# Attention: each row's maximum brought into its row of q by DMA through DRAM in place of transposes and copies, scores 18 pairs of units ahead of the keys in place of 13

## What is computed

```
q, k, v = ...                                   # (4, 12, 513, 16), from a projection of the tokens
a = jax.nn.softmax(jnp.einsum('bhnd,bhmd->bhnm', q, k) * scale, axis=-1)
o = jnp.einsum('bhnm,bhmd->bhnd', a, v)
```

## Time and profile before

| | |
|---|---|
| median of 3 runs | 1972.85 us (1969.68 to 1983.47) |
| the profiled execution | 1996.65 us, span 1994.9 us |
| busy in the span | PE 1500.4, DVE 1375.3, ACT 1074.7, POOL 315.6 us |
| attention in the second layer | about 890.7 to 1077.3 us of the span |
| attention in the last layer | about 1631 to 1817.6 us of the span |
| granted TensorE clock, mean of the span | 0.82 |

### The profile page before, as it was taken

The page is one execution under the profiler, slowest core; times in us unless marked ns, Lnnn a source line. Parts: engine busy times, 40 slices in busy tenths (PEclk is TensorE's granted clock), DMA queues, the critical chain, the costliest instruction groups (busy, mean ns, idle before and its releaser), DMA issues. The chain is left out here.

```text
span 1994.9 us, 35648 instructions
## 1 busy us (share of the span) xinstructions
PE 1500.4 (75%) x13740; PEld 1117.2 (56%) x13740; DVE 1375.3 (69%) x2930; ACT 1074.7 (54%) x1862; POOL 315.6 (16%) x396
## 2 busy tenths in 40 slices
PE   5899993954499849599998504888059599998596
PEld 5888992954366627464445503877047454445274
DVE  6988984798457545649994676776465559993466
ACT  7988992322545326347985425555000438894365
POOL 0000000002567210120000102776000220000100
PEclk9999995876558759698997656999578789997598
DMA  4111001000000010000000333111100000000100
GB/s 128 37 49 33 2 1 44 1 4 1 1 1 1 7 30 1 9 1 1 2 2 5 104 96 110 55 57 52 65 13 0 10 1 2 2 2 4 30 1 32
DMA packets 44499, 49.78 MB, mean 25 GB/s; under 512 B 11000, under 2 KB 37334, under 8 KB 44332
## 3 DMA queue, kind: packets, MB, share of 16 engines
q1 hardware_dynamic: 38354, 32.61, 5.8%
q0 software_dynamic: 3840, 9.18, 1.5%
q10 hardware_dynamic: 2138, 5.72, 1.2%
HBM read 38.32 MB, written 9.19 MB: 24 GB/s over the span
## 5 line engine op out<-in xcount | busy, mean ns | idle before, releaser
L1879 DVE TENSOR_REDUCE att_max<-banks 104x1 f32<-104x512 f32 (+1 forms) x480 | 296.0, 682 | 15.4 <-PE banks L1794 11.3
L1914 ACT ACTIVATE att_p<-banks 104x514 f32<-104x514 f32 (+1 forms) x480 | 261.8, 599 | 35.6 <-PE banks L1837 25.5
L332 PE MATMUL banks<-tok_wT,feature_halves 128*128 128x192 f16 x2592 | 228.0, 248 | 23.4 <-DVE feature_halves L358 12.3
L332 PEld LDWEIGHTS banks<-tok_wT,feature_halves 128*128 128x128 f16 x2592 | 216.0, 99 | 32.4 <-DVE feature_halves L358 18.1
L1853 PE MATMUL banks<-att_p,att_v 104*32 104x257 f32 (+1 forms) x1920 | 163.1, 413 | 0.6
L1837 PE MATMUL banks<-att_q,att_kT 64*104 64x257 f16 (+1 forms) x960 | 156.2, 307 | 2.6 <-ACT att_p L1914 2.5
L1794 PE MATMUL banks<-att_kT,att_q 64*104 64x512 f16 (+1 forms) x480 | 127.7, 428 | 10.1 <-POOL att_last_keys L1764 8.0
L358 DVE TENSOR_TENSOR feature_halves<-features,feature_halves 128x2048 f16<-128x2048 f32 x54 | 123.3, 2284 | 5.5 <-ACT feature_halves L455 5.5
L1837 PEld LDWEIGHTS banks<-att_q,att_kT 64*104 64x104 f16 (+1 forms) x960 | 61.8, 124 | 107.7 <-ACT att_p L1914 80.4
L455 ACT CAST feature_halves<-features 128x2048 f16<-128x2048 f32 x54 | 102.2, 1893 | 9.9 <-PE banks L332 9.1
L2664 DVE COPY expert_w<-expert_weights 128x1536 f32 x80 | 72.3, 907 | 9.3 <-DVE slot_y L2690 7.3
(11 more groups left out here) (462 smaller groups left out, 3525.4 us busy)
## 6 DMA issues: line engine op xcount, KB each, us to landing
tok_w<-in_L_tok_W_dram ACTq DMA_DIRECT2D x4, 1152.0 KB, 7.3
moe_w_in<-in_L_ffn_w_dram SPq DMA_DIRECT2D x8, 576.0 KB, 5.8
expert_y<-expert_out SPq DMA_DIRECT2D x6, 513.0 KB
moe_w_in<-in_L_ffn_w_dram SPq DMA_DIRECT2D x8, 384.0 KB, 3.6
moe_w_in<-in_L_ffn_w_dram SPq DMA_DIRECT2D x16, 192.0 KB, 4.6
raw<-in_x_dram SPq DMA_DIRECT2D x2, 1152.0 KB, 5.3
token_rows<-moe_rows SPq DMA_DIRECT2D x6, 342.0 KB
raw<-in_x_dram SPq DMA_DIRECT2D x2, 896.0 KB, 15.1
```

The source lines that it names most:

```text
L332: ins = pe.matmul(c.bank[t // 2][:, (t % 2) * D:(t % 2 + 1) * D], fh[:, s, q, z, t * 128:(t + 1) * 128], wT[:, y, k, 6 * q + wf, :], start ...
L1879: dve.reduce_max(mx[0:qn, n // NS % 2, 2 * gi + e, k:k + 1], bank_of(unit)[0:qn, 0:ROW], X).then_inc(maxed, 1)
L1914: act.activation(p[0:kn, n % 4, :, :], c.pair[2 + n % 2][0:kn, :].rearrange("p (e q) -> p e q", e=2)[:, :, 0:HALF], ACT.Exp, scale=scale). ...
```

## The change

The maxima are written as fp16 halves, queries on partitions, four heads by five tiles in 20 columns (`m16`, `att_max_halves`). SP writes them to a DRAM tensor `rows` (`att_max_rows`), each element to the place at which it lies in its head's row, waits for that write, and reads two pieces of two rows of 513 back into partitions 32 and 96 of `q2`. PE waits for both reads (`moved`) at a group's first key unit. `turn`, `copy_max`, the identity and the memset of `mexp` are gone, and `LEAD` is `PAIRS + 8`. The buffer of the maxima is free again when the write has landed (`listed`).

```diff
-        mexp = c.sb(ctx, name + "_max_placed", [128, 2, 2, NK, 128], F16)
+        m16 = c.sb(ctx, name + "_max_halves", [128, 2, 2, 2, NK], F16)
-        idh = c.sb(ctx, name + "_ident", [128, 128], F16)
...
+        listed, moved = ([c.sem(f"{name}_max_{q}{k}") for k in range(2)] for q in ("listed", "moved"))
+        rows = nc.dram_tensor(name + "_max_rows", (G, 4, NK * QT), F16, kind="Internal").ap()
...
-        LEAD = PAIRS + 3
+        LEAD = PAIRS + 8
...
-            ring += [("max", g - 1, 0), ("max", g - 1, 1)] if u == 1 and g else []
...
-        def copy_max(eng, copy, g, gi, e):
...
-            copy(q2[r:r + 1, 2 * j + gi, b * T:(b + 1) * T], bank[r:r + 1, 0:T]).then_inc(mc[e], 1)
...
+            @block.sync
+            def _(sp):
+                for g, (b, j) in enumerate(groups):
+                    sp.wait_ge(placed, 2 * g + 2)
+                    sp.dma_start(rows[g].rearrange("h (k p) -> p (h k)", p=QT), m16[0:QT, g % 2, :, :, :].rearrange(
+                        "p e i k -> p (e i k)"), allow_slow_non_contiguous=True).then_inc(listed[g % 2], 16)
+                    sp.wait_ge(listed[g % 2], 16 * (g // 2 + 1))
+                    for e in range(2):
+                        r = 64 * e + 32
+                        sp.dma_start(q2[r:r + 1, 2 * j:2 * j + 2, b * T:(b + 1) * T],
+                                     rows[g:g + 1, 2 * e:2 * e + 2, 0:T]).then_inc(moved[g % 2], 16)
+                for k in range(2):
+                    sp.wait_ge(moved[k], 32 * (G // 2))
...
-                pool.tensor_copy(idh[:, :], c.const("ident")).then_inc(init, 1)
-                pool.memset(mexp[:, :, :, :, :], 0.0).then_inc(init, 1)
...
-                def turn(g):
-                    pe.wait_ge(placed, 2 * g + 2)
-                    for gi in range(2):
-                        free(("max", g, gi))
...
-                            ins = pe.transpose(bank[:, q0:q0 + qn], mexp[0:qn, g % 2, gi, k, :], idh[0:qn, 0:qn])
-                        ins.then_inc(mt, 1)
...
-                    if i < 2:
-                        for e in range(2):
-                            pe.wait_ge(mc[e], 2 * g + gi + 1)
+                    if i == 0:
+                        pe.wait_ge(moved[g % 2], 32 * (g // 2 + 1))
...
                         if g >= 2:
-                            dve.wait_ge(mt, 2 * (g - 1))
+                            dve.wait_ge(listed[g % 2], 16 * (g // 2))
...
-                            dve.tensor_tensor(mexp[0:QT, g % 2, :, :, 64 * x + 32], a, b_, ALU.max
+                            dve.tensor_tensor(m16[0:QT, g % 2, x, :, :], a, b_, ALU.max
                                               ).then_inc(placed, 1)
-                    else:
-                        copy_max(dve, dve.tensor_copy, unit[1], unit[2], 0)
...
-                for gi in range(2):
-                    copy_max(act, act.copy, 0, gi, 1)
...
-                    if i == NB - 3 and g + 1 < G:
-                        for gi in range(2):
-                            copy_max(act, act.copy, g + 1, gi, 1)
```

More of the change, by code:

```diff
@@ L1715, in attention @@
         mx = c.sb(ctx, name + "_max", [128, 2, 4, NK])
-        mexp = c.sb(ctx, name + "_max_placed", [128, 2, 2, NK, 128], F16)
+        m16 = c.sb(ctx, name + "_max_halves", [128, 2, 2, 2, NK], F16)
         p = c.sb(ctx, name + "_p", [128, 4, 2, HALF])
-        idh = c.sb(ctx, name + "_ident", [128, 128], F16)
         last = c.sb(ctx, name + "_last_keys", [128, HEADS // 2, BATCH, 2], F16)
[L1720 to L1723, removed]
+        names = ("_set", "_scored", "_last_scored", "_maxed", "_placed", "_keyed", "_exp", "_summed", "_sums_copied")
+        init, scored, lasts, maxed, placed, keyed, expd, summed, copied = (c.sem(name + x) for x in names)
+        listed, moved = ([c.sem(f"{name}_max_{q}{k}") for k in range(2)] for q in ("listed", "moved"))
+        rows = nc.dram_tensor(name + "_max_rows", (G, 4, NK * QT), F16, kind="Internal").ap()
         S_UNITS = [(gi, k, e) for gi in range(2) for k in range(NK) for e in range(2)]
@@ L1767, in _ @@
             def _(pe):
-                pe.wait_ge(init, 6)
+                pe.wait_ge(init, 4)
                 def free(unit):
@@ L1777, in free @@
                         pe.wait_ge(maxed, before[1] + 1)
-                    elif before[0] == "last":
+                    else:
                         pe.wait_ge(placed, 2 * before[1] + 2)
-                    else:
-                        for e in range(2):
-                            pe.wait_ge(mc[e], 2 * before[1] + before[2] + 1)
                 def score_pair(s):
@@ L1805, in last_keys @@
                     ins.then_inc(lasts, 1)
-                def turn(g):
-                    pe.wait_ge(placed, 2 * g + 2)
-                    for gi in range(2):
-                        free(("max", g, gi))
-                        bank = bank_of(("max", g, gi)).bitcast(F16)
-                        for k in range(NK):
-                            q0, qn = KT[k]
-                            ins = pe.transpose(bank[:, q0:q0 + qn], mexp[0:qn, g % 2, gi, k, :], idh[0:qn, 0:qn])
-                        ins.then_inc(mt, 1)
                 def others(s):
@@ L1821, in others @@
                         last_keys(g)
-                    if u == 1 and 1 <= g <= G:
-                        turn(g - 1)
                 def keys(n):
@@ L1880, in _ @@
                                        ).then_inc(maxed, 1)
-                    elif unit[0] == "last":
+                    else:
                         g = unit[1]
```

11 lines of the change are left out of this document (2 added, 9 removed).

## The result

The changed kernel takes 2190.24 us (median of 4 runs, 2187.30 to 2203.87), the kernel before 1978.16 (median of 4): 1.109 times as long, 95% interval 1.103 to 1.115. It is slower by 212 us, where 17 us less were forecast, and far outside the range.

The account below looks back on a forecast made before the run. DVE and PE were taken to bound the kernel in step. Per stage, 2.4 (later keys) - 16.8 (steady part) + 6.1 (longer end) + 0 (DRAM) = -8.3, for two -16.6 against 1972.85: 1956.3 us, range 1944 to 1997.

Parts of the forecast that it names:

- The write: SP's store of each group's maxima into DRAM: forecast to land in 3.8 to 8.3 us, lower half taken.
- The chain in all: Write, then reads back, until PE's first keys: 6.3 or 10.8 us, taken under 9.2, so 0 added.
- cover: Time in a group from placed maxima to the keys that want them: 9.2 us, 8.0 for the first group.
- Rival B: The DRAM chain comes out and PE waits at each group's first keys: 1997 us; chance 0.25.
- the same two rows: Trace rows giving the write's packet bounds: 8.7 ns from 4-byte reads, 36.9 ns from the nearest store.
- the sum: Both attention stages: 2.4 - 16.8 + 6.1 + 0 = -8.3 us each, -16.6 in all.
- Its dearest case: Write of 320 packets an engine at 36.9 ns: chain 16.7 us, kernel over 2100 us.
- The engines: The write to DRAM: 13 DMA engines with eight partitions each, 160 packets an engine.
- the steady part: Scores beside keys in a stage: 131.0 us against 147.8, -16.8, with 12.58 a group on PE.
- The end of a stage: Keys alone after the scores, five pairs more, partly at clock 0.50: 28.5 us against 22.4, +6.1.
- rival C: Clock stays up or falls later in the keys-alone part, and DVE's 12.36 a group holds: 1943 us; chance 0.12.
- rival D: Removed work was hidden after all, a group falls only to about 13.2 us: 1969 us; chance 0.11.

Follow-up runs that it names:

- run 5: The changed kernel with its 2,080 2-byte pieces written 64 bytes apart in DRAM instead of side by side; 2350.73 us.
- run 9: The kernel of run 1 with one more waited-for write per group, in twelve forms of piece size, spacing and count; these landed in 3.7 to 14.5 us.
- run 1: The changed kernel with maxima first turned in 32 x 32 blocks on DVE, written by four DMAs in runs of up to 64 bytes; 1963.63 us.
- run 6: The changed kernel with its write cut in two, partitions 0 to 99 and 100 to 103; 2136.82 us.
- run 2: The kernel before with scores 18 pairs ahead in place of 13 and ACT's copies moved, nothing by DMA; 2000.74 us, ratio 1.010.
- run 11: The kernel of run 1 with scores 15 pairs ahead in place of 18; 1961.15 us, ratio 0.986.
- run 12: The kernel of run 1 with scores 14 pairs ahead in place of 18; 1980.97 us, ratio 0.998.
- run 8: The kernel of run 1 with one more waited-for write per group, 2,080 zeros of 2 bytes to an unused place; 2187.13 us.

## Why the prediction was wrong, point by point

- **The write, the step that failed.** I took a fixed part of 2.4 us plus packets at 8.7 to 36.9 ns, 3.8 to 8.3 us, and the lower half of that. It takes 14.4. The packets were priced well (11.0 ns each in the trace). The fixed part was not: I took it from a store of rows of 768 bytes, and here the time from the last packet until the write counts as done is 11.6 us alone. It goes with 32 pieces lying in each 64 bytes of DRAM, and is gone when they lie 64 bytes apart (runs 5 and 9). I had written down that every write lies in the same 4 KB, and drew no bound from it.
- **The chain in all.** 14.4 + 2.4 = 16.8 us against a cover of 9.2. The 2.4 to 2.5 us of the reads were right, and in run 1 the cover too (9.1 us from the end of the placing, 936.71, to the keys, 945.82). In the changed kernel slow pairs stretch it to some 11.1 (930.44 to 941.53, where PE stops), which is why PE stands for 5.6 us and not 7.6.
- **Rival B had the mechanism**, down to the waits of line 1822, but its 1997 us came from the same two rows as the sum. Its dearest case, a chain of 16.7 us and over 2100, was met by luck, at a price that is none of its own: not more packets an engine, but near neighbours.
- **What a wait costs.** I named a lower clock behind such waits, and put down the wait alone. Of the 9.6 us that a group is longer, 7.9 are the longer way from write to keys and 1.8 the pairs and last keys at the lower clock between those keys and the next write.
- **The engines.** The trace counts 2,093 packets for the 2,080 pieces of a write; I read the 13 more as one for the semaphore from each of 13 engines. It decided nothing: cut for ten engines and four, with 2,094 packets, the write was no slower (run 6).
- **The steps around it held.** POOL released the first score 2.4 us earlier (PE's wait for the last keys fell from 4.01 us to 1.59). In run 1 a group is 12.56 against 12.58, the keys start 21.0 us after the first score against 21.2, and the steady part is 132.8 and 134.1 against 131.0. That 131.0 counts one last keys too many, 0.58 us, which stands again in the end part, so the gap is that much wider than it looks; it lies in the first groups.
- **The end of a stage** was mis-sized: 23.3 in run 1, against 28.5, since the clock stayed up (rival C's condition). It did so in both stages of runs 1, 2 and 11 (18 and 15 pairs ahead, with ACT's copies and without), and fell in both before and in one of run 12. What decides it stays open. In the changed kernel it was 0.50 at the end of both stages, behind the last group's wait.
- **All in all,** with a write that lands in 2.35 us the sum comes near: -22.4 us in run 1 (1963.63 against 1986.07 beside it; by the interval -11 to -29), -16.6 forecast. In part two misses cancel there: over both stages the end is 10.4 us shorter than forecast and the steady part 4.9 longer. With 12.56 us a group, rival D, which wanted about 13.2, is out.

On rival B's rule, from the Trainium skill, *DMA: Bandwidth & Descriptors*, "Specifications" (below 512 bytes a transfer is done as read-modify-write): smallness by itself was not dear here, since the 2,080 2-byte pieces 64 bytes apart of run 9 land in 4.1 us, where a store of 512 rows of 768 bytes took 3.8. That pieces which must rewrite a common place come one after the other would go with that rule and with the times of close pieces; that this is the mechanism is argued, not shown.

## What to carry to other kernels

A DMA's packets in a trace are not its duration: take it from its issue to what waited for it, and if no DMA of the same pattern stands in the trace, leave its price open upward. A scatter of small elements that interleave in DRAM is priced by how many of them fall close together; here, turned in SBUF first and written in runs of up to 64 bytes, the write landed in 2.4 us in place of 14.4. A wait on TensorE can cost more than itself where the clock falls behind it, here 1.8 us a group.

## What the runs showed of the hardware that I had not expected

- 2,080 writes of 2 bytes into 4 KB of DRAM: packets gone after 3 us, landed after 12.6 to 15.3. The same 64 bytes apart: 3.4 to 4.3.
- Written to DRAM at equal distance, pieces of 2 and 4 bytes cost nearly the same (7.3 to 7.5 us against 7.7 to 8.0 at 4 bytes apart); read into one partition of SBUF, 513 of 2 bytes take 6.6 to 8.0 us and 513 of 4 bytes 3.7 to 4.7, and the distance matters little.
- Why the changed kernel's own write takes 14.4 us and the same form with zeros 12.6 to 13.7 (runs 8 and 9) is open.
- The clock at the end of a stage stayed at 1.00 in runs 1, 2 and 11, and fell to 0.50 before: 5 us of a stage's end, for a reason that these runs don't show.
